# Attention over four key segments on one core: ScalarE's work is put in TensorE's order, and the context's load is issued ahead of a store

## What is computed

```python
q = _heads(hidden_states @ to_q_w)
h_txt = _sdpa(q, _heads(ehs_txt @ to_k_w), _heads(ehs_txt @ to_v_w))
h_obj = _sdpa(q, _heads(ehs_obj @ to_k_object_w), _heads(ehs_obj @ to_v_object_w))
h_oth = _sdpa(q, _heads(ehs_oth @ to_k_others_w), _heads(ehs_oth @ to_v_others_w))
h_ip = _sdpa(q, _heads(ehs_ip @ to_k_ip_w), _heads(ehs_ip @ to_v_ip_w))
out = _merge(h_txt) + SCALE_OBJ * _merge(h_obj) + SCALE_OTH * _merge(h_oth) + SCALE_IP * _merge(h_ip)
out = out @ to_out_w + to_out_b
out = (out + residual) / RESCALE
```

## Time and profile before

| | before |
|---|---|
| median of 3 runs | 1683.23 us |
| profiled execution, its own time | 1681.79 us |
| its span in the profile | 1679.6 us |
| busy: PE / PEld | 1571.8 / 1416.0 us |
| busy: DVE / ACT / POOL | 1399.0 / 1271.1 / 1448.2 us |
| DMA engines, share of the span | 85.6% |
| granted TensorE clock, mean | 0.995 |

### The profile page before, as it was taken

One profiled execution on the slowest core, in us unless ns is written; L12 is line 12 of the kernel. 1 busy time (PEld: TensorE's weight loads), 2 busy tenths in 40 slices (PEclk: granted clock), 3 DMA queues, 4 the chain that ended last, 5 costly groups with the idle time before them and its releaser, 6 DMA issues.

```text
span 1679.6 us, 51529 instructions
## 1 busy us (share of the span) xinstructions
PE 1571.8 (94%) x16252; PEld 1416.0 (84%) x16252; DVE 1399.0 (83%) x3359; ACT 1271.1 (76%) x2416; POOL 1448.2 (86%) x1646
## 2 busy tenths in 40 slices
PE   6879999999999999999999999999999999999976
PEld 3568888899888889888888988888898888899865
DVE  3358888988888898888888888889888888988896
ACT  1247888887887887788788778878877888887765
POOL 3459899989989999998998998999899899989865
PEclk9989999999999999999999999999999999999999
DMA  8688989988988988898898889899889989988961
GB/s 308 175 219 197 217 233 243 216 217 220 240 211 228 250 197 232 217 242 211 234 239 205 231 215 231 221 239 231 209 227 223 219 230 242 216 219 224 218 143 34
DMA packets 423237, 366.26 MB, mean 218 GB/s; under 512 B 19041, under 2 KB 394274, under 8 KB 418850
## 3 DMA queue, kind: packets, MB, share of 16 engines
q1 hardware_dynamic: 423202, 365.80, 85.6%
HBM read 216.38 MB, written 149.34 MB: 218 GB/s over the span
## 4 chain that ended last, share of the span: by engine, by line
PE 76%; ACT 10%; issue 7%; DVE 3%; POOL 1%; DMA 1%; SPq 1%; ACTq 1%; POOLq 0%
PE job_ps L934 16%; PE ring_ps L1012 13%; PE ring_ps L1035 10%; PE ring_ps L1025 10%; PE job_ps L921 9%; PE s_ps L985 6%; PE job_ps L960 5%; ACT probs L644 3%; ACT pT L656 2%; PE ring_ps L885 2%; PE job_ps L963 2%; ACT v_new L602 1%; PE job_ps L944 1%; DVE l_seg L797 1%; ACT c L624 1%
## 5 line engine op out<-in xcount | busy, mean ns | idle before, releaser
L526 POOL TENSOR_TENSOR probs<-probs,rl 128x616 f32<-128x616 f32 (+1 forms) x640 | 629.2, 1005 | 65.7 <-DVE rl L808 65.3
L797 DVE TENSOR_REDUCE l_seg<-probs 128x8 f32<-128x616 f32 (+1 forms) x640 | 386.5, 646 | 137.2 <-ACT probs L644 137.1
L656 ACT ACTIVATE pT<-ring_ps 128x512 f32<-128x512 f32 x640 | 373.4, 603 | 164.2 <-PE ring_ps L1012 160.1
L1012 PE MATMUL ring_ps<-ident,probs 128*128 128x128 f32 x2560 | 389.6, 277 | 11.2 <-DVE y_all L819 8.7
L770 DVE TENSOR_TENSOR probs<-s_ps,m_seg 128x616 f32<-128x616 f32 (+1 forms) x640 | 387.8, 649 | 0.0
L754 DVE TENSOR_REDUCE m_seg<-s_ps 128x8 f32<-128x616 f32 (+1 forms) x640 | 371.5, 623 | 3.5 <-issue 0.2
L644 ACT ACTIVATE probs<-probs 128x1024 f32<-128x1024 f32 x320 | 341.3, 1067 | 7.9 <-DVE probs L774 7.9
L1012 PEld LDWEIGHTS ring_ps<-ident,probs 128*128 128x128 f32 x2560 | 290.1, 143 | 44.7 <-issue 25.0
L934 PE MATMUL job_ps<-c,w 128*128 128x312 f32 x1860 | 304.7, 313 | 0.9 <-POOL c L507 0.9
L934 PEld LDWEIGHTS job_ps<-c,w 128*128 128x128 f32 x1860 | 272.5, 190 | 1.3 <-POOL c L507 1.3
L1035 PE MATMUL ring_ps<-w_o,oT 128*128 128x320 f32 x1152 | 202.6, 320 | 47.5 <-ACT pT L656 45.1
(11 more groups left out here) (69 smaller groups left out, 2047.9 us busy)
## 6 DMA issues: line engine op xcount, KB each, us to landing
q_all<-q_scratch SPq DMA_DIRECT2D x64, 960.0 KB, 7.9
k_all<-k_scratch SPq DMA_DIRECT2D x64, 960.0 KB, 12.3
c_in<-in_cT SPq DMA_DIRECT2D x32, 1024.0 KB, 5.7
x_raw<-in_xT SPq DMA_DIRECT2D x32, 768.0 KB, 7.2
q_scratch<-parts SPq DMA_DIRECT2D x64, 384.0 KB, 4.7
k_scratch<-parts SPq DMA_DIRECT2D x64, 384.0 KB, 5.5
x_res<-in_x SPq DMA_DIRECT2D x128, 160.0 KB, 3.5
out<-y_all SPq DMA_DIRECT2D x128, 160.0 KB, 3.3
```

What stands on the lines that cost most here:

```text
L526: pool.tensor_tensor(pr[:, :, a:e], pr[:, :, a:e], r[:, :, s:s + 1].broadcast_to((P, OH, e - a)), ALU.mult)
L656: act.activation(pT[:, h:h + QH, :], ring_ps[i][:, :].rearrange("p (h s) -> p h s", h=QH), ACT.Copy)\
L797: dve.tensor_reduce(l_seg[:, o % 2, :, s:s + 1], pr[:, :, a:e], axis=AX.X, op=ALU.add)
L1012: last = pe.transpose(ring_ps[i][:, k * S:(k + 1) * S], probs[:, (o % NR) * OH + q * QH + k, :], ident[:, :])
```

## The change

ScalarE's emptying of banks and its part 2 roundings go into a function `free_banks`. In slots without a "y" it stands where they stood; in slots with one (1, 3, 6, 8) it follows the copy of the first transposes. The job that ended in the slot's first piece is emptied between the copies of the two transposes, not after both. The context is rounded on ScalarE in slots 4 and 5, one half each, not both in 5; GpSimd's half of it stays where it was. In SyncE's pass `load_c` and `load_small` stand in front of the store of "kv 2" and of the output of batch -2.

```diff
-CHI_AT, CLO_AT = [5, 5], [5, 6]
+CHI_AT, CLO_AT = [4, 5], [5, 6]
...
                 if live(g + 1, G):
                     store_parts(g + 1, 4)
-                    store_parts(g + 1, 5)
-                finish(g, -2)
                 if live(g + 2, G):
                     load_c(g + 2)
                     load_small(g + 2)
+                if live(g + 1, G):
+                    store_parts(g + 1, 5)
+                finish(g, -2)
                 if live(g + 1, G):
                     load_pair(g, 1, 0)
...
-            def slot(g, n):
-
-                if live(g, G):
-                    exponent(g, n)
+            def free_banks(g, n):
+
                 for turn, job in ended(g, n - 1, 1):
                     evacuate(turn, job)
                 for at in range(2):
                     for turn, job in ended(g, n - 2 - at, at):
                         if job in SPLITS:
                             round_second(turn + 2, SPLITS.index(job))
+
+            def slot(g, n):
+
+                if live(g, G):
+                    exponent(g, n)
+                if n not in PROJECT_AT:
+                    free_banks(g, n)
...
-                    if kind == "tr" and what[1] == 0 and n in VALUES_AT and live(g * NB + VALUES_AT[n], B):
-                        oT_high(g * NB + VALUES_AT[n])
-                for turn, job in ended(g, n, 0):
-                    evacuate(turn, job)
+                    if kind == "tr" and what[1] == 0:
+                        if n in PROJECT_AT:
+                            free_banks(g, n)
+                        if n in VALUES_AT and live(g * NB + VALUES_AT[n], B):
+                            oT_high(g * NB + VALUES_AT[n])
+                        for turn, job in ended(g, n, 0):
+                            evacuate(turn, job)
```

## The result

The changed kernel takes 1628.75 us, the median of 4 runs (1628.05 to 1630.69), beside 1683.59 for the kernel before on the same chip: a ratio of 0.9674, 95% interval 0.9656 to 0.9691. That is 55 us less. The forecast was 67 less, 1616, in a range of 1604 to 1649. So the direction and the mechanism held, and a fifth of the gain did not come. The profiled execution took 1628.05 us around a span of 1625.8.

A forecast was written before the change was run, and what follows sets the result against it. TensorE was taken as the bound, with stalls in slots 6 and 8. 1.14 + 0.72 + 0.38 = 2.24 us per pass over 30 passes gives 67 us, so 1683.2 - 67 = 1616 us, range 1604 to 1649.

The forecast's parts named there:

- What bounds the kernel, and counting from start to start: TensorE sets the pace; its stalls per pass, counted between starts, are 2.52 us, not the idle column's 1.79.
- the prize was 76: All three stalls per pass in slots 6 and 8 removed: 30 x 2.52 = 76 us.
- Slot 6: At slot 6's "y", ScalarE's copy comes earlier: of a 1.38 us delay 1.14 goes.
- the rest of 0.24: Part of the stall at slot 6's "y" forecast to stay, in us per pass.
- Slots 7 and 8: Emptying "kv 0" at once removes 0.72 us at slot 8's "kv 1" and 0.38 at its "y".
- The five edits at no price: ScalarE's waits for a job before the second copy, slots 2, 3, 5, 6, 7: taken as 0 per pass.
- The load: Context load issued 4.3 us earlier, landing with 1.5 us of slack; half stack 0.4 to 1 later but hidden.
- It decides from a landing of 9.4 us on: Slower rival, 5%: ScalarE stands still in slot 4 for a late context; longest landing loses 4.2 per pass, 1808 us.
- All of it: Rival, 12%: copies come a little sooner than worked out, the whole 76 us goes, 1608 us.
- A store keeps a bank: Rival, 15%: "kv 0"'s second copy waits for "q 0"'s last store, 0.7 us lost per pass, 1637 us.
- Another engine becomes the bound: Rival, 10%: GpSimd keeps 3.2 us idle per pass, pass 48.2, gain 32 us, 1651 us.

The follow-up runs named there:

- e6: Changed kernel with both the edits of e4 and e5: 1616.16 us, ratio 0.9601 to the kernel before.
- e5: Changed kernel with ScalarE's second rounding of the context at the end of slot 6, not of 5: 1627.84 us, ratio 0.9670.
- e4: Changed kernel with, in slot 7, GpSimd's third part of "q 1" in front of the scaling of octet 6: 1619.16 us, ratio 0.9620.
- e2: Changed kernel with SyncE's old order, so the context's load is late, roundings still in slots 4 and 5: 1757.35 us, ratio 1.0428.
- e3: Changed kernel with SyncE's old order (late load) and both context roundings in slot 5: 1650.29 us, ratio 0.9805.
- e1: Kernel before with SyncE's new order alone, the context's load in front of the store of "kv 2": 1683.65 us, ratio 0.9999.

## Why the prediction was right, and where it was off

*What bounds the kernel, and counting from start to start.* Right. The idle column had offered 54 us at most; by starts the prize was 76, and e6 took 67 of it. Adding up idle time would have called e6 impossible. After the change the column shows no stall at all in a pass, and the starts still show 0.7 us of them. The Trainium skill (Perfetto Trace Analysis, "Tensor Engine Instruction (MATMUL, LD_WEIGHTS)") says that TensorE's end is computed from the instruction's size and not observed; these 0.7 us without an idle time agree with it.

*Slot 6.* Right to the hundredth: 0.60 us forecast between the starts, 0.59 measured. Why the rest of 0.24 stays was only half understood: it was put down to ScalarE's list, and e5 shows 0.17 of it to be the way from the transposes over the copy to "y".

*Slots 7 and 8.* This is the step that was mis-sized. It said: "Now it empties it at once: 829.33 to 830.3. 'kv 1' wants its bank ...: no stall, and the whole 0.72 goes", and of "y" that some 0.04 stays. The copy waits for two things: the job, and the third part of the split job two before it, whose buffer it takes. The order rows shown with the change had it in print, `L613 ACTIVATE whole<-job_ps 128x512 [waits part3_made]`; I walked ScalarE's list against TensorE and not against GpSimd. e4 prices it at 0.36 us per pass; with what is left at "y" in e4, 0.07 more (0.47 for 0.40), that is the 0.42 that did not come.

*The five edits at no price.* Bounds of -0.3 to 0.7, taken as 0. Nothing in the traces asks for another value: e4 leaves 47.09 - 47.03 = 0.06 for all of them and every other error.

*The load.* Right: landed 1.5 us ahead of need (5.6 us after issue, 838.05 - 836.5). The half stack went out some 1 us later (1.0 at the median, 1.4 in the pass shown) and stayed hidden. "It decides from a landing of 9.4 us on" was not tested as such, but e2 shows the mechanism at work and its sum too low. By that sum a wait of 3.2 us costs 3.2 - 2.24 = 1.0 per pass against the kernel before; e2 lost 52.03 - 49.27 = 2.8. The 1.8 between them is what the clock costs in e2, and the rival left it out.

*The rivals.* "All of it" did not happen. "A store keeps a bank" is real but belongs to the kernel without the early load (e3). "Another engine becomes the bound" was the nearest: not because GpSimd's time ran out, but because one of its results came late in a list that had been late enough for it before. I had put its price (32 us of gain left) on its load; the real thing is one exchange of two instructions.

## What to carry to other kernels

When a list is reordered so that an instruction starts earlier, write down every semaphore it waits for, and when each is met, not only the one that released it in the trace before: the others were hidden behind it. Count the stalls of a pipelined engine from start to start against an unstalled pair of the same instructions; the idle column can be empty while most of a microsecond per pass is lost. And an edit that is worth nothing alone (an earlier load) can be what another one stands on: take it out of the finished kernel too, not only put it into the old one.

## What the hardware showed that was not expected

A late transfer costs more than its lateness: 3.2 us of wait per pass in e2 made passes 3.4 to 6.7 us longer than in the changed kernel, in part by TensorE's clock. It fell behind 28 of 29 stalls, down to one of 2.09 us, and not behind one of 2.11, so the length of the stall alone does not say whether it falls. And SyncE itself stands still while it issues: the half stack's k part of 960 KB took 4.27 us to issue behind the context and q's part. In e1, whose only edit is SyncE's new order, the same issue takes 1.34, and in the changed kernel 1.42; the output of 160 KB behind it still takes 4.62, before 4.75 (SyncE's timeline, e1 and then the changed kernel):

```profile
815.55 1.34 SPq L367 DMA_DIRECT2D k_all<-k_scratch  x1
```
```profile
838.38 1.42 SPq L367 DMA_DIRECT2D k_all<-k_scratch  x1
840.00 4.62 SPq L380 DMA_DIRECT2D out<-y_all  x1
```
